# Sign matrix of a gated layer: raw signs rounded by ScalarE in the block stage instead of rounded signs stored in attention

## What is computed

```
x = x + tanh(g_xattn) * xattn(layernorm(x), ...)
x = x + tanh(g_ffn)   * einsum('bsi,io->bso', layernorm(x), sign) * softplus(scale)
```

## Time and profile before

| | us |
|---|---|
| median of 3 runs (2185.62 to 2191.09) | 2190.39 |
| the profiled execution, its own time | 2187.38 |
| its span in the profile | 2185.6 |
| TensorE matmul busy in the span | 1952.4 (89%) |
| VectorE busy | 1326.9 (61%) |
| ScalarE busy | 872.6 (40%) |
| GpSimd busy | 489.5 (22%) |
| HBM read / written | 323.79 / 139.20 MB |

### The profile page before, as it was taken

The page is one execution under the profiler, slowest core; times in us unless marked ns, Lnnn a source line. Parts: engine busy times, 40 slices in busy tenths (PEclk is TensorE's granted clock), DMA queues, the critical chain, the costliest instruction groups (busy, mean ns, idle before and its releaser), DMA issues.

```text
span 2185.6 us, 25302 instructions
## 1 busy us (share of the span) xinstructions
PE 1952.4 (89%) x9818; PEld 1336.6 (61%) x9818; DVE 1326.9 (61%) x1399; ACT 872.6 (40%) x1184; POOL 489.5 (22%) x370
## 2 busy tenths in 40 slices
PE   4789987989999983499999999999999999989997
PEld 0344455545555542278677777677777677666776
DVE  5476667556666639769468458567558567567110
ACT  4646652556666643162362440262530261432000
POOL 0022344787566620000000001100011100011010
PEclk8889997999999996699999999999999999989999
DMA  7548357999999714347467658677658667668675
GB/s 263 157 114 226 115 152 179 311 280 326 269 261 279 234 68 170 140 149 289 165 264 261 242 155 237 189 277 284 227 139 239 203 261 283 241 155 233 157 178 132
DMA packets 156477, 464.75 MB, mean 213 GB/s; under 512 B 34370, under 2 KB 35010, under 8 KB 138946
## 3 DMA queue, kind: packets, MB, share of 16 engines
q1 hardware_dynamic: 123760, 324.19, 47.6%
q0 software_dynamic: 30432, 128.46, 19.1%
q10 hardware_dynamic: 2160, 10.43, 1.3%
HBM read 323.79 MB, written 139.20 MB: 212 GB/s over the span
## 4 chain that ended last, share of the span: by engine, by line
PE 41%; DMA 8%; DVE 7%; ACT 4%; issue 2%; SPq 0%; POOL 0%; DVEq 0%; POOLq 0%; ACTq 0%
PE ps L1820 15%; PE ps L1630 8%; PE ps L1632 7%; PE ps L1631 7%; DMA sign_h<-sign_h_scratch 5%; DMA up<-up_s_scratch 2%; PE ps L1689 1%; PE ps L1698 1%; ACT L1849 1%; PE ps L1650 1%; DVE Y L2143 1%; PE ps L1739 1%; PE ps L1727 1%; DVE E_attn L2055 0%; ACT E_attn L1873 0%
## 5 line engine op out<-in xcount | busy, mean ns | idle before, releaser
L1820 PE MATMUL ps<-XH,sign_h 128*128 128x512 f32 x768 | 310.9, 405 | 19.9 <-DMA sign_h<-sign_h_scratch 15.3
L1820 PE MATMUL ps<-XL,sign_h 128*128 128x512 f32 x768 | 303.9, 396 | 0.0
L1197 DVE TENSOR_REDUCE maxes<-ps 128x1 f32<-128x512 f32 (+3 forms) x384 | 207.7, 555 | 146.6 <-PE ps L1051 112.3
L1630 PE MATMUL ps<-ZH,up 128*128 128x512 f32 x512 | 204.4, 399 | 16.9 <-DVE ZL L2168 8.9
L1147 ACT ACTIVATE probs<-ps 128x512 f32<-128x512 f32 (+3 forms) x384 | 168.6, 489 | 126.2 <-PE ps L1078 83.9
L1632 PE MATMUL ps<-ZH,up 128*128 128x512 f32 x512 | 200.4, 391 | 0.0
L1631 PE MATMUL ps<-ZL,up 128*128 128x512 f32 x512 | 200.4, 391 | 0.0
L1820 PEld LDWEIGHTS ps<-XH,sign_h 128*128 128x128 f32 x768 | 147.1, 191 | 68.6 <-DMA sign_h<-sign_h_scratch 18.3
L1820 PEld LDWEIGHTS ps<-XL,sign_h 128*128 128x128 f32 x768 | 147.2, 192 | 32.1 <-issue 1.9
L1093 PE MATMUL ps<-probs,values 128*32 128x512 f32 (+3 forms) x768 | 164.5, 503 | 0.1
L1093 PE MATMUL ps<-probs,ones_sum 128*32 128x512 f32 (+3 forms) x768 | 164.5, 503 | 0.0
(11 more groups left out here) (333 smaller groups left out, 4132.8 us busy)
## 6 DMA issues: line engine op xcount, KB each, us to landing
sign_h<-sign_h_scratch SPq DMA_DIRECT2D x256, 256.0 KB, 4.3
up<-up_s_scratch SPq DMA_DIRECT2D x58, 1024.0 KB, 6.2
proj<-proj_s_scratch SPq DMA_DIRECT2D x58, 640.0 KB, 3.9
X<-in_x_read POOLq DMA_DIRECT2D x16, 1024.0 KB, 9.0
xn_scratch<-X SPq DMA_DIRECT2D x16, 1024.0 KB, 14.2
sign_raw<-in_sign SPq DMA_DIRECT2D x32, 512.0 KB, 9.8
sign_h_scratch<-sign_high SPq DMA_DIRECT2D x32, 512.0 KB, 8.6
up_s_scratch<-weight_split SPq DMA_DIRECT2D x16, 1024.0 KB, 9.1
```

Of the source, the lines that this page charges most:

```text
L1197: eng.tensor_reduce(MAXES[:, e, q, k0 // T:k0 // T + 1], ps[:, ring_bank(n, ("max", m)), 0:w], AX.X, ALU.max).then_inc(mx_read.sem, mx_rea ...
L1630: eng.matmul(out_ap, lh, rh, start=start, stop=False, skip_group_check=True)
L1820: mm = eng.matmul(ps[:, sign_bank(m)], s[q][:, f], x[:, n], start=n + w == 0, stop=n == NF - 1 and w == len(operands) - 1, skip_group_chec ...
```

## The change

Attention still rounds the signs to find out whether they have a low rest, but no longer stores them; SP's loads of the next raw signs and weights wait directly for POOL where its stores did. In the block phase SP loads raw signs from the input: block 0 of stages 0 to 2 into the place of `SH` itself, all others into a second set of four tiles (`sign_raw_to_cut`), which was used before for the low rest alone. A fetch waits until the first matmul of the same quarter of block m - 1 is done (`s_raw_free`). A new part of ScalarE's program, `sign_highs`, rounds each quarter into `SH` when it has landed (`s_in`) and when the matmuls that read the old contents are done (`ffn`); TensorE waits for it (`s_high`). The steps that ScalarE did on its own in the stages now stand between its roundings by two new tables. VectorE's table for stages 0 and 1 moves the scaling of blocks 2 and 3 one step ahead.

```diff
@@ attention, SP
                 def load_weights(e, n):
+                    past(eng, probed, n - 1, 2 * e + 2)
                     eng.dma_start(SIGN[e][:], io["sign"][n:n + 1, :, e * HF:(e + 1) * HF].rearrange("a p f o -> (a p) f o")
                                   ).then_inc(sign_in[e].sem, sign_in[e].unit)
+                    past(eng, weight_cut, n - 1, 2 * e + 2)
                     eng.dma_start(WRAW[e][:], io[("mlp_up", "mlp_proj")[e]][n:n + 1].rearrange("a p n -> (a p) n")
                                   ).then_inc(weight_in[e].sem, weight_in[e].unit)
 
                 def store_weights(e, n):
-                    eng.wait_ge(probed.sem, probed.at(n, 2 * e + 2))
-                    eng.dma_start(io["sign_h"][n:n + 1, :, e * HF:(e + 1) * HF].rearrange("a p f o -> (a p) f o"), SIGN_H[e][:].bitcast(F32)
-                                  ).then_inc(sign_out[e].sem, sign_out[e].unit)
                     eng.wait_ge(weight_cut.sem, weight_cut.at(n, 2 * e + 2))
@@ attention, end of SP's list; POOL's probe
-                    eng.wait_ge(sign_out[a].sem, sign_out[a].at(PAIRS - 1))
-                    past(eng, sign_out[e], n - 1)
@@ block phase
-        SRAW = [in_s(f"sign_again{q}", 8 + 2 * q, [P, FQ, P]) for q in range(NQ)]
+        SRAW = [in_s(f"sign_raw_to_cut{q}", 8 + 2 * q, [P, FQ, P]) for q in range(NQ)]
+        SRAW_0 = [in_s(f"sign_raw_in_place{q}", 2 * q, [P, FQ, P]) for q in range(NQ)]
+
+        def sign_raw(u, m):
+            return SRAW_0 if m == 0 and u < LAST else SRAW
@@ SP
                 def load_sign(u, m):
+                    if m == 1 and u < LAST - 1:
+                        eng.wait_ge(yl.sem, yl.at(u + 2))
+                    elif m == 1 and u == LAST - 1:
+                        eng.wait_ge(x2.sem, x2.at(u, 4))
                     for q in range(NQ):
                         if m:
-                            eng.wait_ge(ffn.sem, ffn.at(u, m * NQ - NQ + q + 1))
+                            eng.wait_ge(s_raw_free.sem, s_raw_free.at(u, m * NQ - NQ + q + 1))
                         elif u == LAST:
-                            eng.wait_ge(ffn.sem, ffn.at(u - 1, NF * NQ - NQ + q + 1))
+                            eng.wait_ge(s_raw_free.sem, s_raw_free.at(u - 1, NF * NQ - NQ + q + 1))
                         else:
                             eng.wait_ge(x2.sem, x2.at(u, 3))
-                        eng.dma_start(SH[q][:].bitcast(F32), io["sign_h"][m, :, q * FQ:(q + 1) * FQ]).then_inc(s_in[q].sem, s_in[q].unit)
+                        eng.dma_start(sign_raw(u, m)[q][:], io["sign"][m, :, q * FQ:(q + 1) * FQ]).then_inc(s_in[q].sem, s_in[q].unit)
@@ TensorE, signs
                             for q in range(NQ):
-                                eng.wait_ge(s_in[q].sem, s_in[q].at(u, m + 1))
+                                eng.wait_ge(s_high.sem, s_high.at(u, NQ * m + q + 1))
...
+                                        if w == 0 and f == (FQ - 1 if with_low else 0):
+                                            mm.then_inc(s_raw_free.sem, s_raw_free.unit)
@@ ScalarE
+                def sign_highs(u, between):
+                    for m in range(NF):
+                        for q in range(NQ):
+                            eng.wait_ge(s_in[q].sem, s_in[q].at(u, m + 1))
+                            if m:
+                                eng.wait_ge(ffn.sem, ffn.at(u, m * NQ - NQ + q + 1))
+                            elif u == LAST:
+                                eng.wait_ge(ffn.sem, ffn.at(u - 1, NF * NQ - NQ + q + 1))
+                            eng.activation(SH[q][:], sign_raw(u, m)[q][:], ACT.Copy).then_inc(s_high.sem, s_high.unit)
+                            between.at(NQ * m + q)
+                    between.rest()
...
+                IN_SIGNS = (2, 6) + (10, 10, 11, 11, 11, 12, 13, 14, 15, 17, 22) + (52, 53, 55, 56, 58, 59)
+                AT_LAST = (7, 8, 8, 9, 10, 11, 12, 13, 14, 16, 23) + (42, 44, 44, 45, 46, 47, 48, 49, 50, 55, 57)
...
                     if u + 2 < NB:
-                        Between(first_write(u + 2), ()).rest()
-                Between(second_write(LAST), ()).rest()
+                        sign_highs(u, Between(first_write(u + 2), IN_SIGNS))
+                sign_highs(LAST - 1, Between(second_write(LAST), AT_LAST))
+                sign_highs(LAST, Between(iter(()), ()))
@@ VectorE
-                IN_SIGNS = (0,) + (1,) * 7 + (2, 2, 2, 2, 3, 3, 3) + (3, 3, 4, 4, 4, 5, 5) + (6, 6, 6, 7, 7, 8) + (8, 8, 9, 9, 9, 10) + (
+                IN_SIGNS = (0,) + (1,) * 7 + (2, 2, 2, 3, 3, 3, 3) + (4, 4, 4, 4, 5, 5, 5) + (6, 6, 6, 7, 7, 8) + (8, 8, 9, 9, 9, 10) + (
```

More of the change, by code:

```diff
@@ L871, in attention_phase @@
         sign_in = [ev(f"sign_in{a}", unit=16) for a in range(2)]
-        sign_out = [ev(f"sign_out{a}", unit=16) for a in range(2)]
         weight_in = [ev(f"weight_in{a}", unit=16) for a in range(2)]
@@ L1372, in block_phase @@
             (("x2", 4), ("mean", 2), ("c", 4), ("xh", 4), ("sq", 4), ("xl", 4), ("v", 5), ("rs", 1), ("gate", 1)))
-        s_in, l_raw = ([ev(f"{n}_in{q}", per=NF, unit=16) for q in range(NQ)] for n in ("sign_h", "sign_again"))
+        s_in = [ev(f"sign_in{q}", per=NF, unit=16) for q in range(NQ)]
+        l_raw = ev("sign_again_in", per=NQ, unit=16)
+        s_high, s_raw_free = ev("sign_high", per=NQ * NF), ev("sign_raw_free", per=NQ * NF)
         l_in = ev("sign_l_made", per=NQ * NF)
@@ L1520, in low @@
                     def low(u, m):
[L1521 to L1534 removed]
+                        again = m == 0 and u < LAST
+                        for q in range(NQ if with_low and again else 0):
+                            if u < LAST - 1:
+                                eng.wait_ge(yl.sem, yl.at(u + 2))
+                            else:
+                                eng.wait_ge(x2.sem, x2.at(u, 4))
+                            eng.sem_inc(pool_turn.sem, 1)
+                            eng.dma_start(SRAW[q][:], io["sign"][m, :, q * FQ:(q + 1) * FQ]).then_inc(l_raw.sem, l_raw.unit)
+                        for q in range(NQ if with_low else 0):
+                            if again:
+                                eng.wait_ge(l_raw.sem, l_raw.at(u, NQ))
+                            eng.wait_ge(s_high.sem, s_high.at(u, NQ * m + q + 1))
                             eng.tensor_tensor(SL[q][:], SRAW[q][:], SH[q][:].bitcast(F32), ALU.subtract).then_inc(l_in.sem, l_in.unit)
@@ L1928, in first_write @@
                         take_y(v)
+                        yield
                         take_walls(v)
+                        yield
                     yield from write(s, 0, first[v], (F0,) if v == 1 else (X0, X1))
@@ L2273, in build @@
     io["x_read"] = args["x_read"].rearrange("n a p (j t) -> n a p j t", j=C)
-    for name, shape in (("up_s", [NM, P, 2, 2 * HC * P]), ("proj_s", [NM, P, 2, WALL]), ("wall_s", [P, HC, 2, WALL]),
-                        ("sign_h", [NF, P, NF, P])):
+    for name, shape in (("up_s", [NM, P, 2, 2 * HC * P]), ("proj_s", [NM, P, 2, WALL]), ("wall_s", [P, HC, 2, WALL])):
         io[name] = nc.dram_tensor(name + "_scratch", shape, F32, kind="Internal").ap()
```

14 lines of the change are left out of this document (1 added, 13 removed).

## The result

| | before | changed |
|---|---|---|
| median (4 runs each, in one series), us | 2188.01 (2182.91 to 2191.09) | 2229.14 (2219.37 to 2233.52) |
| ratio, 95% interval | | 1.0191 (1.0164 to 1.0218) |
| the profiled execution, its own time / span | 2187.38 / 2185.6 | 2233.52 / 2231.7 |
| HBM read / written, MB | 323.79 / 139.20 | 323.79 / 122.42 |

The change costs 41 us, 1.9%. I had said 2208, at most 2226: the sign was right, the size was less than half of what came.

The account below looks back on a forecast made before the run. TensorE was taken to bound the kernel, with 21 us of sign-load waits and clock loss to gain. Attention -1.5, stage 0 +11, stage 1 +8.6, stages 2 and 3 +1.8 sum to +19.9: 2208 us stated, range 2182 to 2226.

Parts of the forecast that it names:

- The load's cover: Sign stages: fetch starts 1.6 us earlier but a rounding intervenes; cover grows from 5.44 to about 6.4 us, 0.9 per load.
- its load waits go, -4.5: Stage 3: ScalarE has no other work there, so the waits for sign loads vanish, -4.5 us.
- 2.5 us of lead: Stage 0, middle: quarters land 4.3 us after their fetch, so ScalarE can round about 2.5 us ahead of use.
- Start of the stages: Stages 0 to 2: first rounding waits behind ScalarE's closing steps; 4.2 us idle plus 1.6 clock, net +5.1, +5.1, +4.3.
- Stage 0, middle: Stage 0 up to Y: roundings among ScalarE's steps delay VectorE and TensorE; Y at 123.9 instead of 116.2, +7.8 us.
- end: Stage 0 after Y: the square stands behind rounding 52 and four weight-load issues, 3.8 us idle; +3.2 us in all.
- Attention: Attention phase: without 32 sign stores only the 7.8 us wait for `first_k` can shrink; -1.5 us, bounds 0 and -4.
- theory B: Attention: for f1, longer at 1.2 GHz, +3 to +7 us; for f2, changed attention costs about 5, 2222 to 2226.
- Rival C: Attention was bound by its DMA share, so dropping the stores gives -57 us, 2133; chance 0.02.
- A: Sign stages: loads stop showing and ScalarE's order never bites, only the starts cost; -8 us, 2182; chance 0.13.
- B: Sign stages: starts cost, but the second Exp or the square is covered in two stages; 2197 (+7); chance 0.22.
- D: Sign stages: loads land later than 4.3 us; at 6 us, +6 per stage with chain, 2226; chance 0.13.

Follow-up runs that it names:

- h2: Kernel before, with the store of wall_s and the load of expand in attention moved behind the next pair's operand loads: 2182.83 us, ratio 0.9987.
- f3: Changed kernel with the attention phase of before, sign stores included, and the block phase loading the stored signs from scratch: 2227.12 us, ratio 1.0181.
- f2: Changed kernel with the attention phase of before, sign stores and their waits included, though nothing reads them: 2225.28 us, ratio 1.0176.
- g3: Changed kernel, SP refilling a raw buffer once ScalarE has rounded its contents, not after TensorE's first matmul on the rounded copy: 2197.21 us, ratio 1.0050.
- h1: Changed kernel with the edits of f4 and g3, without g1's: 2180.40 us, ratio 0.9994.
- f4: Changed kernel, with ScalarE's block 0 roundings in stages 0 to 2 moved ahead of `small_1` and `out_sb`: 2207.44 us, ratio 1.0109.
- g1: Changed kernel with three ScalarE table entries moved: the Exp of `E_attn` three roundings later, the two squares two quarters ahead: 2217.37 us, ratio 1.0149.
- h3: Changed kernel with all edits of g4 plus h2's move in attention: 2165.52 us, ratio 0.9920.
- f1: Kernel before with signs stored for the first pair only, every block reading block 0's signs: 2192.26 us, ratio 1.0025.
- g4: Changed kernel with the edits of f4, g1 and g3 together: 2177.11 us, ratio 0.9954.
- h4: Changed kernel, ScalarE rounding only one of each quarter's four tiles from block 1 on, the rest left stale: 2219.44 us, ratio 1.0163.

## Why the prediction was wrong

**The sum.** Stages: predicted +11, +8.6, +6.3, -4.5 = 21.4; measured +11.9, +10.7, +9.4, +4.5 = 36.5. Of the miss of 15.1, 9.0 is stage 3, 3.1 stage 2, 2.1 stage 1 and 0.9 stage 0. The median's 41.1 exceeds the sum of 19.9 by 21.2; the other 6.1 are 1.7 of attention (predicted -1.5, left over 0.2) and 4.4 of the two `inner` phases, in which little of the change lies and which scatter by as much in h2.

**"The load's cover": half right, and the step that failed.** The cover itself came out nearly as worked: 14.5 - 7.8 - 0.7 = 6.0 us in the loop above, 1.0 more than the 5.0 of before, where I said about 6.4 and 0.9 more. But I compared it with the median landing, 4.3 (after: 4.1), and concluded that "its load waits go, -4.5" in stage 3, and that the load waits go in stages 1 and 2. Those waits were never made by the median load. They came from the loads that land last, 5.4 to 5.8 us in the chain of before in stage 3, and these land 6.4 to 7.7 us after the fetch now: the cover gained 1.0 us, they lose 1 to 2. f3 excludes the source of the loads, f2 the stores in attention. Why they land later was not found: that such loads are fetched right behind POOL's stores is read from the timelines, holds before as well, and was not varied; that a cover of 6 us doesn't hold them, while g3's does, is shown. The prediction had the earlier trace rows with 12.8 as the longest and should have set the cover against the loads in the chain, not against the middle of the list.

**What follows from it in the stages with a chain.** I gave ScalarE's queue 2.5 us of lead. That holds for a landing of 4.3; behind a load of over 6 us it has none, and every step after that rounding is late with it. Stage 2 shows where this hurts. `x_last` releases TensorE 63.5 us into the stage, 57.4 before: +6.1, where I had 6.5. From there to stage 3 it takes 99.4 us against 96.1: +3.3, where I had 2.0 - 2.2 = -0.2, and this is the stage's miss. `rstd_gate_last`, which I did not list, stands in ScalarE's queue behind two roundings whose loads were late (3.14 us), and a sign matmul at 2019.48 waits 1.36 us for its rounding. In g3 neither wait is there; by the fetch alone it takes 10.4 us out of stage 2, 8.2 of them behind `x_last`, so the mechanism is shown; the shares of the single waits are only read.

TensorE's longer waits for VectorE in this stage are another matter: 5.08 us at `x_last`, where it had waited 3.13, and 4.16 at `product_scaled`. g3 has 5.08 and 3.69 of them, and h1, whose stage 2 is 4.9 us shorter than before's, has the same (of its timeline):

```profile
1952.91 1.94 PE L1732 MATMUL ps<-x_last,ones_p 128*32 128x512 f32 x8 [5.09 <-DVE x_last L2221]
```

There TensorE comes to `x_last` earlier and VectorE no later than before (57.2 us into the stage), so the longer wait by itself is not what the change costs.

**"Start of the stages": right.** 4.12 us idle and half clock, as said (4.2 and 1.6); f4 takes 14.8 us out against 14.5 predicted.

**"Stage 0, middle" and "end": right in sum, roughly in parts.** Predicted and found: TensorE's tenth expansion waits longer (3.19 us against 4.0); quarter 23 waits for its rounding (3.48 against 4.2); Y's sum is late by 9.4 us from the stage's start (125.6 against 116.2) where I had 7.8; the square 2.42 against 3.8; from Y to the stage's end +2.5 (45.9 against 43.3) where I had 3.2. The terms I gave for that end add up to 2.5 to 2.8, not 3.2, a slip that made the sum larger. Stage 1 had the same waits (3.20, 2.31, 2.13) and was 2.1 us longer than predicted, f2's and f3's 4.8 and 4.7. I had let its load waits go; how much of them came back as waits for ScalarE's roundings is not shown, since besides the start and quarter 23 these make 1.1 us of idle time. g1 shows that the waits behind the table are no prices to be added: with the Exp out of the way a slow load cost as much in its place.

**"Attention": not to be told from zero.** I said -1.5. The medians of f2 and of the changed kernel, which differ in the stores, are 2225.3 and 2229.1 with overlapping intervals. In the profiles, h2 and h3 left aside, `inner(1)` ends between 1248 and 1264 us in kernels without the stores and at 1256, 1259 and 1257 in those with them. The changed kernel's 5.2 us lie inside that scatter. That leaving out the stores costs a few us is not excluded either: f1 (+5.5 us by its ratio) and f2 (2225) both lie where theory B had put them, and f3, with the stores as well, took 2227. Rival C is refuted: the DMA share of the earlier trace rows fell from 0.97 to 0.90 and 293 to 223 GB/s, TensorE stayed at 99.68 of 100 us.

**The rivals.** A (the loads stop showing), which is also the rule to double-buffer in the Trainium skill (Trainium Kernel Development and Optimization, Best Practices), did not come true here but does in g3, g4 and h3, where stage 3 takes 117.1 us (I had 118 for it) and, in h3, the sign group idles 6.7 us. I was right that this change gets less than a second buffer from it, and wrong on what "in part" costs. Against A I also argued that VectorE's product would be late before rounding 23 whatever the landing, and that held. g3 has that wait (2.32 us at 1334.88), and so has h1, without the late start:

```profile
1317.58 0.50 PE L1825 MATMUL ps<-XH,sign_h 128*128 128x512 f32 x1 [2.11 <-ACT sign_h L2017]
```

In g4, where the Exp stands three roundings later, at most 0.6 us is left of it. B (the Exp before rounding 23 or the square covered after all) did not come true: both waits were there in both stages. D (loads land later, about 6 us, 2226) was nearest; it had the landing right for the slow loads and was given 0.13. The range ended at D's time and took in neither D with the load waits still there nor any scatter of the profile it was built on.

## What to carry to other kernels

A second buffer in front of a conversion helps as far as its fetch is tied to the conversion, not to the consumer behind it: count the loop fetch, landing, conversion, first use, and set what is left against the slow loads that stand in the chain of waits, never against the median landing. An engine that gets a new duty in the middle of a stage has its old steps delayed by every late input of the new one; give it a lead first, then tune its places (here 28 us for the earlier fetch, 3 to 9 for the places behind it). At a stage's start, put the new duty ahead of the old stage's closing steps.

## What the runs showed of the hardware

Behind the 3.48 us of 1338.16 they do so from the third one, and behind the 3.19 us of 1319.61 not at all (0.23), while the kernel before had half clock behind 2.48 us. The same wait of 2.17 us for VectorE's `product_scaled` early in stage 2 had half clock behind it within eight matmuls in the profiles of the kernel before and of the changed one, and not in the other twelve.

In the changed kernel a 256 KB load landed in 2.9 us at best and 4.1 in the median; in g1 one took 10.35 us right behind two of POOL's stores.

More surprising is attention. Behind nearly the same wait for `first_k` (7.78, 6.66 and 7.2 us) the kernel before was back at full clock by 455 us, the changed one was not, and g1, whose attention is the changed kernel's, was. First before, then changed, then g1 (columns as in the earlier trace rows):

```profile
455.00:470.00 15.00, 14.92 (x110) 7.97 (x108) 10.15 (x20) 9.27 (x19) 13.58 (x8) 1.00 1.01 290
```

```profile
455.00:470.00 15.00, 15.00 (x76) 8.52 (x75) 7.20 (x15) 5.36 (x11) 14.60 (x9) 0.55 0.94 248
```

```profile
455.00:470.00 15.00, 14.93 (x112) 8.29 (x104) 9.99 (x20) 9.26 (x19) 14.69 (x8) 1.00 0.95 248
```

TensorE is busy in all three, 14.92 to 15.00 of 15 us, and does 110, 76 and 112 matmuls. So this differs from execution to execution and is not the change's: of the ten profiles with a wait of 5.7 us or more, three have the low clock in this stretch, the changed kernel's, h4's (0.52) and also f2's (0.57), whose attention is that of before. It may be most of the 5.2 us by which the changed kernel's block phase begins later: from 446 to 480 us it does 184 matmuls where the kernel before does 225, by an estimate from these two counts 6 us. In h2, h3, f4 and h1, where the wait is gone or under 1 us, the clock from 446 to 480 us is 1.00. What decides how long the lower level lasts was not tried, nor was the one small edit of VectorE's table tested by itself.
